# Attention with a sparse mask: row shuffles one step later, products thirteen steps behind, scatter bounds kept in registers

## What is computed

```
x = x + gnn(layernorm(x), adj)        # then the experts:
x = x + moe(layernorm(x))

# gnn: keys are cut into 8 chunks of 128; the softmax is taken inside each chunk
scores = clip(q @ k_chunk.T / sqrt(32), -10, 10); scores = where(mask == 0, -10, scores)
attn   = softmax(scores, axis=-1)     # over the 128 keys of one chunk
ctx    = sum over chunks of attn @ v_chunk
out    = layernorm(ctx @ Wo.T + bo + x)
# moe: gate softmax, top 2 of 8, out = sum of share * (gelu(x @ W1[e] + b1[e]) @ W2[e] + b2[e])
```

## Time and profile before

| | |
|---|---|
| median of three runs | 820.97 us (820.46 to 822.31) |
| the profiled execution | 819.6 us |
| span of its trace | 817.7 us |
| busy share of the span | PE 82%, DVE 84%, ACT 69%, POOL 68% |
| chain that ended last | PE 44%, POOL 17%, DVE 16%, issue 9%, ACT 9%, DMA 3% |
| attention, batches 0 to 7 | from about 35 to 515 us |
| gates, scatters | about 515 to 635 us |
| experts | about 635 to 810 us |

### The profile page before, as it was taken

How to read it: one execution, slowest core, us unless ns; L and a number is a source line. 1 busy time by engine, 2 the same in 40 slices (tenths; PEclk the granted TensorE clock), 3 DMA queues, 4 the chain that set the end, 5 groups by cost and what they waited for, 6 DMA issues and landing times.

```text
span 817.7 us, 20365 instructions
## 1 busy us (share of the span) xinstructions
PE 669.0 (82%) x6427; PEld 387.7 (47%) x6427; DVE 689.7 (84%) x1753; ACT 563.0 (69%) x1091; POOL 556.2 (68%) x571
## 2 busy tenths in 40 slices
PE   4698499999999999999999884756610699999994
PEld 1333134334434334334343322745510599999994
DVE  4989989999999999999999999886670488888893
ACT  4697388997997998989988865525300477777772
POOL 1211718798998997988989999777777055555554
PEclk9799899999999999999999997555655799999997
DMA  8926104536226144153261104001111222222210
GB/s 277 251 85 153 50 25 150 154 104 184 79 97 163 53 133 142 49 163 97 76 166 65 66 1 104 1 27 31 54 52 52 53 66 71 81 82 78 63 48 1
DMA packets 58851, 74.54 MB, mean 91 GB/s; under 512 B 8172, under 2 KB 33609, under 8 KB 58746
## 3 DMA queue, kind: packets, MB, share of 16 engines
q1 hardware_dynamic: 41114, 41.59, 16.9%
q10 hardware_dynamic: 12672, 23.07, 10.7%
q0 software_dynamic: 4960, 8.58, 3.2%
HBM read 52.38 MB, written 22.59 MB: 92 GB/s over the span
## 4 chain that ended last, share of the span: by engine, by line
PE 44%; POOL 17%; DVE 16%; issue 9%; ACT 9%; DMA 3%; SPq 1%; ACTq 1%; POOLq 0%; DVEq 0%
PE score_ps L1532 7%; PE sum_ps L1546 6%; PE side_ps L1562 5%; DVE prob_ring L1013 5%; POOL rows_dram L628 4%; POOL ctx_sb L568 4%; POOL ctx_acc L573 4%; DVE prob_ring L1024 3%; PE score_ps L1490 2%; PE sum_ps L1770 2%; PE sum_ps L1776 2%; PE sum_ps L1772 2%; PE sum_ps L1774 2%; PE score_ps L1492 2%; PE score_ps L1491 2%
## 5 line engine op out<-in xcount | busy, mean ns | idle before, releaser
L1532 PE MATMUL score_ps<-stack_mem 128*128 128x512 f16 x512 | 140.6, 389 | 36.2 <-DVE prob_ring L1013 31.9
L1013 DVE SCALAR_TENSOR_TENSOR w<-score_ps,limit 128x1024 f32<-128x1024 f32 x128 | 150.1, 1215 | 13.9 <-PE score_ps L1532 13.7
L1013 DVE SCALAR_TENSOR_TENSOR prob_ring<-score_ps,limit 128x1024 f32<-128x1024 f32 x128 | 150.3, 1216 | 10.9 <-PE score_ps L1532 9.9
L782 ACT ACTIVATE prob_ring<-prob_ring 128x1024 f32<-128x1024 f32 x128 | 133.9, 1053 | 36.0 <-DVE prob_ring L1013 36.0
L568 POOL TENSOR_TENSOR ctx_sb<-ctx_sb,rspread 128x512 f32<-128x512 f32 x108 | 139.4, 1291 | 21.3 <-POOL ctx_acc L573 10.2
L635 POOL DMA_INDIRECT out_x<-xn,limit x91 | 89.7, 986 | 87.1 <-DVE xn L1387 72.0
L782 ACT ACTIVATE w<-w 128x1024 f32<-128x1024 f32 x128 | 133.7, 1051 | 17.2 <-DVE w L1013 13.9
L573 POOL TENSOR_TENSOR ctx_acc<-ctx_acc,ctx_sb 128x512 f32<-128x512 f32 x93 | 119.7, 1287 | 7.3
L907 ACT ACTIVATE xn<-score_ps,vec 128x128 f32<-128x128 f32 x364 | 99.1, 383 | 11.4 <-PE score_ps L1492 10.3
L1532 PEld LDWEIGHTS score_ps<-stack_mem 128*128 128x128 f16 x512 | 37.6, 98 | 136.3 <-DVE prob_ring L1013 53.8
L628 POOL DMA_INDIRECT rows_dram<-x,limit x64 | 63.2, 988 | 20.8 <-issue 19.7
(11 more groups left out here) (238 smaller groups left out, 1581.4 us busy)
## 6 DMA issues: line engine op xcount, KB each, us to landing
rspread<-rinv_dram SPq DMA_DIRECT2D x70, 256.0 KB
stack_mem<-qk_dram ACTq DMA_DIRECT2D x56, 256.0 KB, 4.8
ctx_sb<-rows_dram SPq DMA_DIRECT2D x91, 66.5 KB, 1.9
qk_dram<-qk_hi ACTq DMA_DIRECT2D x16, 256.0 KB, 2.8
qk_dram<-qk_lo ACTq DMA_DIRECT2D x16, 256.0 KB, 5.1
x<-in_adj SPq DMA_DIRECT2D x4, 512.0 KB, 7.5
ctx_sb<-in_adj SPq DMA_DIRECT2D x4, 512.0 KB, 9.9
stack_mem<-qk_dram SPq DMA_DIRECT2D x16, 128.0 KB, 3.5
```

Source lines behind the costliest of these rows:

```text
L782: act.activation(prob_at(s, u), prob_at(s, u), ACT.Exp, scale=1.0 / SCORE).then_inc(exp_done, 1)
L1013: dve.scalar_tensor_tensor(out=prob_at(s, u), in0=score_ps[:, 2 * u:2 * u + 2, :], scalar=-LIMIT * SCORE, in1=limit[:, k:k + 1, half * HAL ...
L1532: ins = pe.matmul(score_ps[:, h, :], kstack[:, par, h, k * P:k * P + P], qstack[:, par, h, half * HALF:half * HALF + HALF], start=True, st ...
```

## The change

There are two edits to the order and one to the indirect DMAs.

- The spread of a step stands `GROUP + 3` = 11 steps behind the scores and no longer 10: the first pair of shuffles of a group is no longer in the step of the reciprocal but in the next one, and the third pair moves one step on as well. In the last batch's table the third entry goes from 9 to 8, so there too the first pair leaves step 2 for step 3.
- GpSimd's products stand 13 steps behind the scores and no longer 12 (`LAG`). The tables of the last batch are as before, and `due` lets its first step take the product that is left over.
- The two bounds are put into registers once, and the MOVE in front of each of the 64 scatters and 91 stores is gone.

```diff
-    LAG = 12
+    LAG = 13
...
-        SPREAD_BY = (7, 8, 9, 11, 13, 15, 17, 18, 19, 20, 21, 22, 23, 24, 25, 26)
+        SPREAD_BY = (7, 8, 8, 11, 13, 15, 17, 18, 19, 20, 21, 22, 23, 24, 25, 26)
...
+            last_row, last_token = [pool.to_reg(n) for n in (DUMMY + P - 1, NB * N - 1)]
+
             def scatter(tiles):
...
-                                            None, bounds_check=DUMMY + P - 1, oob_is_err=False).then_inc(scattered, 16)
+                                            None, bounds_check=last_row, oob_is_err=False).then_inc(scattered, 16)
...
-                                        stage[:, i % AHEAD, :], None, bounds_check=NB * N - 1,
+                                        stage[:, i % AHEAD, :], None, bounds_check=last_token,
...
-                    for n in due(g, GROUP + 2, SPREAD_BY):
+                    for n in due(g, GROUP + 3, SPREAD_BY):
```

## The result

| | before | changed | ratio, 95% interval |
|---|---|---|---|
| median of 10 runs each, us | 821.07 | 818.58 | 0.9964 (0.9947 to 0.9980) |
| lowest to highest, us | 820.18 to 823.37 | 816.16 to 821.23 | |
| profiled execution, us (span) | 819.6 (817.7) | 818.33 (816.2) | |

The change gains 2.5 us; 3.5 were forecast. Two things stand out: the profiled execution gained only 1.5 us in span, and the runs of the changed kernel spread over 5 us where those of the kernel before spread over 3. Of the runs of the experiments two of set 1, one of the kernel before and one of shuffles only, took 1170 and 1173 us at a granted clock of 0.55 and stand in no median.

What follows compares the result with a forecast made beforehand. PE sets the middle batches' pace, DVE close behind; a GpSimd chain from batch 6's moments sets attention's end. -6.3 + 2.8 + 0 = -3.5 us gives 816.1 profiled, 817.5 median; range 815.3 to 819.3, with A, B and D 814.3 to 821.2.

Steps and rivals of the forecast that it cites:

- PE's stall behind the reciprocals: PE's scores waiting for clips behind reciprocals at steps 2 and 10, batches 1 to 6: from 13.0 to 4.6 us.
- 0.56 of the 0.70 stays: Step 2: moving the shuffle pair frees 0.70 us, step 5 takes some back; 0.56 gained at each of six places.
- I take 0.45: Step 10: gain limited by DVE's idle time before the clip of step 14; 0.45 us at each of five places.
- A shuffle that moves inside that stretch moves nothing.: Batch 0, where DVE is busiest with the input's statistics between its clips: later shuffles change nothing there.
- +2.8 us: Last batch: GpSimd's chain behind batch 6's root block holds one more product and sum, 2.8 us later.
- GpSimd's wait ahead of the root block: Step 12 of each batch: GpSimd still waits for DVE's moments, about 2 us instead of 2.82.
- rival C: Step 13: late `ctxT` stops PE, making the kernel slower; 825.3 us at 3.5 us of lateness; chance 0.15.
- The MOVEs: I take 0.: Scatters and stores: removing the MOVEs gains nothing because the sequencer runs ahead; bounds 0 and 1.9 us.
- The stores lie beside PE's work: The 91 stores: their MOVEs were left out of the 1.9 us bound, so no gain from them was counted.
- Rival B: Last batch: the later product costs nothing and the whole 6.3 us arrives; 814.7 us, chance 0.10.
- rival A: Step 5: DVE's stall only moves and gives all 0.70 back; -0.1 us, 820.8, chance 0.18.
- Rival D: Scatters: the MOVEs were on the path, 1.9 us more gain; 815.6 us, chance 0.05.

Runs made afterwards that it cites:

- set 1: First of three follow-up sets, on another chip: the kernel before at 851.56 us, beside kernels with single edits or two edits of the change.
- shuffles only: Kernel before with only the shuffles one step later and the last batch's third table entry changed; products stay at twelve steps: 847.47 us, ratio 0.9952.
- row stores late: Changed kernel with the 29 stores that begin the rows moved from batch 1 to the last batch: 841.97 us, ratio to before 0.9887.
- product-only kernel: Kernel before with only GpSimd's products thirteen instead of twelve steps behind: 855.14 us, ratio 1.0042.
- the three sets: Follow-up measurements of kernels with single or combined edits, each set on one other chip, where the kernel before takes 849 to 852 us.

## Why the prediction came out as it did

The forecast of 817.5 was 1.1 us off. The path to it was partly right, and errors of both signs cancelled, so the nearness of the number is in part luck: on the way the root block of batch 6 came at 419.42 (forecast 417.7), the last sum at 512.99 (511.1), the last scatter at 631.17 (628.6), 1.0 us earlier than before where the sum had 3.5.

- **PE's stall behind the reciprocals.** Right in place; 13.0 us fell to 2.5, forecast 4.6.
- **"0.56 of the 0.70 stays" and "I take 0.45".** Both too small. From step 2 to step 10 it is 27.72 us instead of 28.45, from there to step 2 26.24 instead of 27.10: 0.73 and 0.86 at a place. The clip follows the reciprocal's start by 1.66 us instead of 2.49, so a place offers 0.83, not 0.70: I had taken the 0.74 between two rows and subtracted a start of 0.04, but a clip starts 0.09 before the reciprocal's listed end, and a shuffle doesn't. And DVE's room at steps 5 and 14, 0.39 and 0.41 us of idle, was used up whole: in the changed kernel's batch from 279.37 us on the first row with idle time in front is at 298.05, in step 8, and up to 324.40, in step 15, there is one more, at 300.88. With the row stores late, from the reciprocal of batch 1's step 2 to that of batch 6's step 10 it is 412.70 - 114.83 = 297.87 us, 418.79 - 112.60 = 306.19 before. That is 8.3 us for what I had put at 3.4 + 2.25 = 5.6. Batch 6's root block adds 0.87, forecast 0.7.
- **"A shuffle that moves inside that stretch moves nothing."** Wrong. It starts GpSimd's row later, and that row blocks DVE's small instructions: 1.55 us up to the end of their chain. Of the 1.07 us that arrived in the first pair, 0.31 have nothing to do with it, and 0.80 were given back by PE's clock.
- **What the sum had no term for.** Batch 2, 3.7 us in the first profile, 3.8 to 6.3 in three others with both shuffles and product moved, 1.6 and 2.9 in the two with the shuffles alone. ScalarE's first stall there, 3.27 us, and 1.46 at the second place stood in the trace of before. I had read the DMA queues for what the change moves past them, not for what was already late and only just covered. That is also where the wider spread could come from, which no run settles.
- **"+2.8 us" in the last batch.** Right: 512.99 - 419.42 = 93.57 us against 90.67, +2.9; the product-only kernel has +3.2, and costs 3.6 us in all.
- **GpSimd's wait ahead of the root block.** Forecast 2 us, measured 1.0 to 1.6 from batch 2 on, by the same reason as the shorter period. PE's output product (L1573 before) was not held up by it: rival C did not come.
- **"The MOVEs: I take 0."** Wrong by 0.8 us inside the bounds of 0 to 1.9. The rows of before did not have 0.30 of gap in front of each scatter "throughout": four had more. In a row of scatters they are free: the pitch is 1.28 us with 0.30 of gap as before. Where a scatter follows small instructions the gap fell from 0.62 to 0.55 and twice from 0.53 to 0.16 us. There the sequencer has no lead, as I read it, and the MOVE stood on the path. In this profile the 0.8 was lost again to single scatters that took up to 1.47 us (all 64 took 1.53 us more than before in sum), which also occurs without registers. "The stores lie beside PE's work" held on the first chip and failed on the others, by 3.3 us.

Put together for the first pair: +1.07 in batch 0, -8.5 at eleven places and -0.9 at the root block, +3.7 in batch 2, +2.9 in the tail, -0.1 at the first scatter, -0.8 at three scatters, +1.5 for the longer ones: -1.1, and the row of the last scatter says -1.0. The medians differ by 1 us more than the spans: the profiled execution of before lay 1.5 us under its median, that of the changed kernel 0.25. Rival B, that the product costs nothing, is out, and rival A, that DVE's stall only moves, too. Rival D had the right idea for the chips of the three sets and the wrong place: the stores, not the scatters.

What stays open: why the experts phase takes 23 us more on those chips (the experts' weight loads take 192 ns there as here, the gaps before them are longer; PE's granted clock is 1.00 in that phase in either case, and PE is busy 155.9 of 158 us in the first pair's kernel before, 163.5 of 180 on a set's chip), how the 29 stores lengthen ScalarE's second stall, what sets the moment at which PE's clock returns in batch 0, and what the late stores gave the kernel before.

## What to carry to other kernels

When a change removes a wait that every batch has, look in the trace of before for stalls of other engines that this wait covered; they are the next bound. Here the cover was 4.8 us, 4.7 of it in use; with the change 3.7 us came through, until 29 unrelated stores were moved. When a product is delayed to suit its producer, try the producer's change alone first: here the consumer's own slack would have taken it, and the delay cost 3 us at the end. A constant operand that costs an instruction on the sequencer was free in a row of DMAs and cost 0.37 us where the DMA followed small instructions, so price it at each such place. And compare a stretch behind a long idle time of PE by its clock first: here that alone moved batch 0 by up to 1.6 us between kernels.

## What the runs showed of the hardware

- VectorE instructions of 128x32 floats took 0.19 us alone and up to 1.30 us beside GpSimd's 128x512 instructions of 1.26 to 1.32 us, ending with them.
- A VectorE clip that reads PSUM started 0.09 us before the listed end of the reciprocal ahead of it; a shuffle started 0.04 us behind it. The pair of shuffles cost 0.83 us between them, not the 0.70 of the rows alone.
- Without the MOVE of 29 ns in front of an indirect DMA the gap ahead of the DMA was 0.37 us shorter at two places behind small GpSimd instructions, and the same 0.30 in a row of DMAs.
- Behind 10.2 to 12.2 us without a matrix product PE ran at a granted clock of 0.50, four score products in 2.08 us instead of 1.04; the clock was back at 1.00 between 4.4 and 7.7 us after the clip that ended the pause, 4.4 and 6.2 us in two executions of the same kernel.
- The same kernel took 821 us in the first pair and 849 to 852 us on the three chips of the later sets, with equal periods in attention and the same mean granted clock (0.89 to 0.90).
